# A stage-by-stage fp32 network on one core: convolution by matrix products, read products shared with GpSimd, high and low halves formed from PSUM

## What is computed

```python
def _L1_ffn_ref:      # stage 4: shared plus chosen units, 12 units of 128 hidden
    h = relu(x @ w1 + b1);  y = h @ w2 + b2        # x masked by the choice for 8 of the 12
def _L3_attn_ref:     # stage 7: the scan
    x = resid * rsqrt(mean(resid^2) + EPS) * norm_w
    skip, xe = x @ skip_w.T, x @ in_w.T            # 256 channels
    xc = causal 4-tap convolution of xe along the tokens, by channel, + conv_b
    xs = silu(xc)
    delta = softplus(xs @ wd1.T @ wd2.T + wd2_b);  A = -exp(A_log)
    Bm, Cm = xs @ wb.T, xs @ wc.T                  # 16 of each a token
    h[e,n] = exp(delta[e] * A[e,n]) * h[e,n] + delta[e] * xs[e] * Bm[n]
    y[e] = sum_n h[e,n] * Cm[n];   y = (y + xs * W_D) * silu(skip);  out = resid + y @ out_w.T
def _L3_ffn_ref:      # stage 8: 8 experts of 512 hidden, every token through every expert
    h = relu(x @ W1[e] + b1[e]);  y = gate[e] * (h @ W2[e] + b2[e])
```

## Time and profile before

| | us |
|---|---|
| median of 3 runs (all: 2960.09, 2961.39, 2972.28) | 2961.39 |
| profiled execution, its own time | 2971.4 |
| its span, first to last instruction | 2969.6 |
| mean granted TensorE clock | 0.911 of full |
| stage 4 | 533 to 706 |
| stage 7, the scan alone | 1820 to 2477 |
| stage 8, the experts alone | 2521 to 2950 |

### The profile page before, as it was taken

One profiled execution on the slowest core, in us unless ns is written; L12 is line 12 of the kernel. 1 busy time (PEld: TensorE's weight loads), 2 busy tenths in 40 slices (PEclk: granted clock), 3 DMA queues, 4 the chain that ended last, 5 costly groups with the idle time before them and its releaser, 6 DMA issues.

```text
span 2969.6 us, 34723 instructions
## 1 busy us (share of the span) xinstructions
PE 2466.0 (83%) x12034; PEld 1751.8 (59%) x12034; DVE 2159.7 (73%) x3859; ACT 1261.5 (42%) x2802; POOL 988.2 (33%) x787
## 2 busy tenths in 40 slices
PE   6677778697999999999699995677777775899998
PEld 2554556576888888888567773222222223667676
DVE  6637556897666666665666664788888897799997
ACT  4221232334444444443355554544444443444444
POOL 1000010232222222222045550444444451466664
PEclk8668899898999999999799996888888898999999
DMA  3000000000000000000100000111111120000001
GB/s 164 0 1 1 1 1 1 1 1 15 1 1 1 1 1 1 1 1 1 58 1 1 1 1 15 54 56 51 50 44 56 58 75 1 1 1 1 1 1 29
DMA packets 25136, 55.56 MB, mean 19 GB/s; under 512 B 2544, under 2 KB 6656, under 8 KB 24448
## 3 DMA queue, kind: packets, MB, share of 16 engines
q1 hardware_dynamic: 24928, 53.32, 5.4%
q0 software_dynamic: 32, 0.02, 0.0%
HBM read 50.96 MB, written 2.36 MB: 18 GB/s over the span
## 4 chain that ended last, share of the span: by engine, by line
PE 46%; DVE 27%; issue 13%; POOL 7%; ACT 6%; DMA 0%; DVEq 0%; POOLq 0%; PEldq 0%; PEld 0%; ACTq 0%; SPq 0%
PE ps L190 43%; DVE TMP L206 5%; DVE TMP L2380 5%; PE ps L197 3%; POOL TMPr L210 3%; POOL XT L210 3%; DVE TMP L209 3%; DVE TMPr L206 3%; ACT TMP L201 2%; DVE TMPr L205 2%; POOL TMP L210 2%; DVE XK L206 1%; ACT TMP L202 1%; DVE TMP L207 1%; ACT TMPr L204 1%
## 5 line engine op out<-in xcount | busy, mean ns | idle before, releaser
L190 PE MATMUL ps<-TMPr 128*128 128x512 f32 (+6 forms) x3976 | 1059.5, 412 | 137.5 <-DVE TMP L206 63.4
L190 PEld LDWEIGHTS ps<-TMPr 128*128 128x128 f32 (+4 forms) x3976 | 734.8, 191 | 498.9 <-issue 151.3
L210 POOL TENSOR_TENSOR TMP<-TMP 128x512 f32<-128x512 f32 (+2 forms) x400 | 461.6, 1169 | 961.2 <-ACT TMP L201 443.9
L190 PE MATMUL ps<-TMP 128*128 128x65 f32 (+4 forms) x4320 | 526.3, 289 | 1.2 <-DVE TMP L205 0.5
L190 PEld LDWEIGHTS ps<-TMP 128*128 128x128 f32 (+3 forms) x4320 | 478.9, 191 | 61.7 <-issue 19.9
L201 ACT ACTIVATE TMP<-ps,W 128x256 f32<-128x256 f32 (+2 forms) x560 | 307.5, 590 | 456.6 <-PE ps L190 227.4
L190 PE MATMUL ps<-TMP,W 128*128 128x512 f32 (+5 forms) x720 | 407.7, 691 | 107.4 <-DVE TMP L209 51.4
L206 DVE TENSOR_TENSOR TMP<-ps,TMP 128x512 f32<-128x512 f32 (+1 forms) x514 | 301.0, 611 | 120.3 <-ACT TMP L201 67.3
L190 PEld LDWEIGHTS ps<-TMP,W 128*128 128x128 f32 (+3 forms) x720 | 130.2, 204 | 289.6 <-issue 213.9
L210 POOL TENSOR_TENSOR TMPr<-XK,TMPr 128x512 fp32r<-128x512 f32 (+1 forms) x132 | 194.7, 1477 | 282.4 <-ACT TMPr L204 282.4
L210 POOL TENSOR_TENSOR TMPr<-TMP,TMPr 128x512 fp32r<-128x512 f32 x96 | 126.6, 1320 | 265.2 <-ACT TMPr L204 265.2
(11 more groups left out here) (172 smaller groups left out, 2924.1 us busy)
## 6 DMA issues: line engine op xcount, KB each, us to landing
TMP<-rows SPq DMA_DIRECT2D x128, 256.0 KB, 3.2
W<-wp SPq DMA_DIRECT2D x1, 4124.0 KB, 13.7
W<-wp SPq DMA_DIRECT2D x1, 3072.0 KB, 25.1
W<-wp SPq DMA_DIRECT2D x1, 2136.5 KB, 18.3
...
```

The costliest lines, as they stand in the source:

```text
L190: return nc.tensor.matmul(out, lhsT, rhs, start=start, stop=stop, **k)
L210: gtt = lambda o, a, b, op: nc.gpsimd.tensor_tensor(o, a, b, op)
```

## The change

It has three parts.

1. **Convolution on TensorE.** The taps are folded into the weights: `Wtap` holds four copies of `in_w`, each multiplied by one tap of each channel (one DMA of the taps and one VectorE product of 1024 columns in the norm stage before the scan). A half's convolution is four fp32 products of shifted columns of `XK` accumulated in PSUM (step "conv", in the same `yield` as "gate"). ScalarE then reads PSUM twice ("conv_out"): `Tanh` with bias, and `Identity` with scale one half and bias. The copies into `xe`, the carried columns and the three taps on VectorE go.
2. **Reading the state.** In the five steps n = 1, 4, 7, 10, 13 of each chunk the read product is on GpSimd, with the row Cm[n] brought to `Cr` (two buffers) by a DMA of its own, issued just ahead of the B row. TensorE's selection falls away in these steps. `rows_d` holds 32 rows a chunk and ScalarE's copy for it has 32 rows, where both had 16.
3. **Stages 4 and 8.** Every unit's relu is on ScalarE and writes the high half at once. Then ScalarE subtracts the bias from the high half into `rb` (`Identity` with the negated bias; in stage 8 every fourth unit has it on VectorE). One VectorE `stt` reads PSUM again and forms the low half, max(PSUM, -b) - `rb`. The PSUM bank is free only after that. GpSimd has no subtraction in units any more.

```diff
+        def sync(e):
+            e.wait_ge(s_fence, 4 * begun)
+            nc.sync.dma_start(Wtap, vecs_d[2:3, :].partition_broadcast(128)).then_inc(s_conv, 16)
...
+            e.wait_ge(s_conv, 16)
+            tt(g3(Wtap, 4), g3(Wtap, 4), w("inT").unsqueeze(1).to_broadcast([128, 4, 256]), ALU.mult).then_inc(*taps_ready("taps"))
...
+        by_pool = lambda g: g % 16 % 3 == 1
...
             yield [("open", (i, 0))]
-            yield [("gate", (i, 0))]
-            yield [("last", (i, 0)), ("open", (i, 1))]
-            yield [("shut", (i, 0)), ("gate", (i, 1))]
-            yield [("last", (i, 1))]
+            yield [("gate", (i, 0)), ("conv", (i, 0))]
+            yield [("conv_out", (i, 0))]
+            yield [("shut", (i, 0)), ("open", (i, 1))]
+            yield [("gate", (i, 1)), ("conv", (i, 1))]
+            yield [("conv_out", (i, 1))]
             yield [("shut", (i, 1)), ("rank", i)]
...
-                    bank_free(e, "in", a)
-                    mm(bank("in", a), tile(inT, x), ch(XK, i)).then_inc(*in_pe(a))
+                elif step == "conv":
+                    i, x = a
+                    bank_free(e, "conv", a)
+                    for back in range(4):
+                        o = 512 * i - back
+                        wt = Wtap[:, (3 - back) * 256 + 128 * x:(3 - back) * 256 + 128 * x + 128]
+                        if i % 2:
+                            r = mm(pr, wt, XK[:, o:o + 512], back == 0, back == 3)
+                        else:
+                            r = mm(pr[:, back:512], wt, XK[:, 512 * i:o + 512], back == 0, back == 3)
...
-                elif step == "decay":
+                elif step == "decay" and not by_pool(a):
...
+                elif step == "conv_out":
+                    i, x = a
+                    e.wait_ge(*cv_pe.at(a))
+                    set_free(e, i)
+                    act(ch(sets[i % 2][1], x), pr, ACT.Tanh, scale=0.5, bias=cb[:, x:x + 1]).then_inc(*xt_act(a))
                     if i:
                         e.wait_ge(*dl_dve.at(i - 1))
-                    act(ch(ev, x), xe[x][:, 0:512], ACT.Identity, scale=cw[:, 4 * x:4 * x + 1], bias=cb[:, x:x + 1]).then_inc(*cv_act(a))
+                    act(ch(ev, x), pr, ACT.Identity, scale=0.5, bias=cb[:, x:x + 1]).then_inc(*ev_act(a))
...
-                    e.wait_ge(*cv_act.at(a))
-                    tap(a, 1).then_inc(*t1_dve(a))
-                    e.wait_ge(*t1_dve.at(a))
-                    tap(a, 2).then_inc(*t2_dve(a))
...
-                    for x in range(2):
+                    for x in range(0 if by_pool(a) else 2):
...
+                elif step == "body" and by_pool(a):
+                    k = pool_turn[a]
+                    e.wait_ge(s_row_c[k % 2], 16 * (k // 2 + 1))
+                    for x in range(2):
+                        q = 2 * a + x
+                        e.wait_ge(*h_dve.at((a, x)))
+                        if a >= 2:
+                            e.wait_ge(*y_pe.at((a - 2, x)))
+                        gtt(Cb[q % 4], Cr[k % 2], Hb[q % 4], ALU.mult).then_inc(*hc_pool((a, x)))
...
+                        if k >= 2:
+                            e.wait_ge(*hc_pool.at((by_turn[k - 2], 1)))
+                        nc.sync.dma_start(Cr[k % 2], rows_d[i, 16 + n:17 + n, :].partition_broadcast(128)).then_inc(s_row_c[k % 2], 16)
```

The same edit in stage 4 (stage 8 has it with `B1`, `nB1` and its own names, and with `ts` on VectorE where `a[3] == 3`):

```diff
-                        e.wait_ge(*relu(back(a, 5)))
+                        e.wait_ge(*low.at(back(a, 5)))
...
+                    act(hb[nth[a] % 6][0], PS[nth[a] % 5], ACT.Relu, bias=bias1(a[1])).then_inc(*high(a))
+                elif step == "parts":
+                    e.wait_ge(*high.at(a))
...
+                    act(rb[nth[a] % 4], hb[nth[a] % 6][0].bitcast(F32), ACT.Identity, bias=nbias(a[1])).then_inc(*q_act(a))
...
+                    stt(hb[nth[a] % 6][1], PS[nth[a] % 5], nbias(a[1]), rb[nth[a] % 4], ALU.max, ALU.subtract).then_inc(*low(a))
```

More of the change, by code:

```diff
@@ L163, in build @@
     s_fence, s_eps = lone("s_fence"), lone("s_eps")
+    s_conv = lone("s_conv")
     s_row, s_row_in = [lone(f"s_row{j}") for j in range(2)], [lone(f"s_row_in{j}") for j in range(4)]
-    rows_d = nc.dram_tensor("rows", (NCH, 16, CH), F32).ap()
+    s_row_c = [lone(f"s_row_c{j}") for j in range(2)]
+    rows_d = nc.dram_tensor("rows", (NCH, 32, CH), F32).ap()
     base = (nc.sbuf_base + 63) // 64 * 64
@@ L1277, in stage4 @@
         back = lambda a, n: order[nth[a] - n]
-        wsum = Sig(sem("s4_sums"), ("gate", "gate high", "gate low", "b2a", "b2"))
+        wsum = Sig(sem("s4_sums"), ("gate", "gate high", "gate low", "b2a", "b2", "nb a", "nb"))
         wpart = Sig(sem("s4_weights"), [(n, s, k) for n in units for s in (0, 1) for k in ("high", "low")])
@@ L1284, in stage4 @@
         up_pe = Sig(sem("s4_up"), order)
-        odd = lambda a: a[1] % 2 == 1
-        r_act, r_dve = Sig(sem("s4_relu_act"), [a for a in order if not odd(a)]), Sig(sem("s4_relu_dve"), [a for a in order if odd(a)])
-        c_act, c_dve = Sig(sem("s4_high_act"), [a for a in order if odd(a)]), Sig(sem("s4_high_dve"), [a for a in order if not odd(a)])
-        third = lambda a: a[1] % 4 == 3
-        s_pool, s_dve = Sig(sem("s4_low_pool"), [a for a in order if third(a)]), Sig(sem("s4_low_dve"), [a for a in order if not third(a)])
+        high, low = Sig(sem("s4_high"), order), Sig(sem("s4_low"), order)
+        q_act = Sig(sem("s4_high_unbiased"), order)
         dn_pe, y_dve = Sig(sem("s4_down"), order), Sig(sem("s4_added"), range(NCH))
-        relu = lambda a: (r_dve if odd(a) else r_act).at(a)
-        high = lambda a: (c_act if odd(a) else c_dve).at(a)
-        low = lambda a: (s_pool if third(a) else s_dve).at(a)
         def pe(e):
@@ L1406, in pool @@
                     gtt(l0x, xl.bitcast(F32), l1x.bitcast(F32), ALU.subtract).then_inc(*l0(a))
-                elif step == "parts" and third(a):
-                    h, l = hb[nth[a] % 6]
-                    e.wait_ge(*high(a))
-                    gtt(l, rb[nth[a] % 4], h.bitcast(F32), ALU.subtract).then_inc(*s_pool(a))
         return dict(pe=pe, dve=dve, act=scalar, pool=pool)
@@ L1929, in expert_stage @@
         bank0 = turns([(s, a) for s, a in plan if s in ("gate", "row")], 1)
-        low = lambda a: (mo_lpool if odd(a) else mo_ldve).at(a)
-        high = lambda a: (mo_hact if k == 6 or odd(a) else mo_hdve).at(a)
+        low = lambda a: (mo_lpool if k == 6 and odd(a) else mo_ldve).at(a)
+        nB1 = SM[:, 340:372]
+        unit = lambda a: slice(4 * a[1] + a[3], 4 * a[1] + a[3] + 1)
         def bank0_free(e, s, a):
@@ L1967, in pe @@
                         if nth[a] >= 5:
-                            o = back(a, 5)
-                            e.wait_ge(*(mo_rdve if odd(o) else mo_ract).at(o))
+                            e.wait_ge(*low(back(a, 5)))
                         mm3(ups[nth[a] % 5], (tile(wh, c), tile(wl, c)), xs).then_inc(*mo_up(a))
@@ L2052, in pool @@
             for step, a in plan:
-                if step == "parts" and odd(a):
+                if step == "parts" and k == 6 and odd(a):
                     h, l = hb[nth[a] % NH]
-                    e.wait_ge(*high(a))
-                    gtt(l, fb[nth[a] % 3] if k == 6 else rb[nth[a] % 4], h.bitcast(F32), ALU.subtract).then_inc(*mo_lpool(a))
+                    e.wait_ge(*mo_high.at(a))
+                    gtt(l, fb[nth[a] % 3], h.bitcast(F32), ALU.subtract).then_inc(*mo_lpool(a))
                 elif step == "down" and a[3] == nd - 1:
@@ L2185, in scan_stage @@
         GE = [(g, e) for g in G for e in range(2)]
[L2186 to L2187 removed]
+        c_pe, raw_act = Sig(sem("s7_c_pe"), [g for g in G if not by_pool(g)]), Sig(sem("s7_b_rows"), I)
+        a_act, u_pool, h_dve, y_pe = (Sig(sem("s7_" + n), GE) for n in ("decay", "input", "state", "y_sum"))
+        hc_dve, hc_pool = (Sig(sem("s7_read_" + n), [(g, e) for g, e in GE if by_pool(g) == p]) for n, p in (("dve", False), ("pool", True)))
+        read = lambda g, x: (hc_pool if by_pool(g) else hc_dve).at((g, x))
         c_act = Sig(sem("s7_carried"), [(g, e) for g, e in GE if g // 16 % 2 == 0])
```

198 lines of the change are left out of this document (89 added, 109 removed).

## The result

The changed kernel takes 2851.4 us (median of 4 runs, 2846.7 to 2854.7) and the kernel before, on the same chip, 2966.8 (2960.1 to 2979.5): a ratio of 0.9605, 95% interval 0.9565 to 0.9645. The profiled execution took 2854.7, with a span of 2852.9 and a mean granted clock of 0.917. Run once more, on another chip, the same kernel gave 0.9574 (0.9554 to 0.9594), so differences of 0.3% between two kernels say little.

A forecast was written before the change was run, and what follows sets the result against it. VectorE was taken to lead in stage 4 and the scan, with TensorE nearly full in stage 8. Scan -84, stage 4 -11, stage 8 -17 took 2971.4 to 2859, lowered for run spread to 2855 us; range 2815 to 2912.

The forecast's parts named there:

- The scan: -84 forecast: Scan: seven chunks 12.0 us shorter each, the last 5.9 shorter, the first preparation 6 longer; -84 us together.
- Collisions, +2.4 forecast: Scan: VectorE instructions with two SBUF inputs lengthen beside GpSimd, both shut and half for dx; +2.4 us a chunk.
- TensorE, +1.0: Scan: the convolution's four fp32 products delay the sums VectorE needs, at low clock; +1.0 us a chunk.
- ScalarE, +1.2: Scan, softplus at step 12: VectorE's cover loses the read product pair of step 13; +1.2 us a chunk.
- GpSimd, 48 a chunk: Scan: GpSimd's products at 1.09 and dx at 2.35 make 48 us of the new chunk, so it has room.
- The start, +6: Scan's first preparation, uncovered at low clock: more fp32 products, tap folding, a first C row; +6 us, between 0 and +12.
- Stage 4: -11 forecast: Stage 4: TensorE stays first and its seven holes of 1.67 go, -11.7, with +0.5 back; -11 us.
- stages 4 and 8 give nothing: Rival, chance 0.08: ScalarE's work reaches TensorE's in stage 4, or the copy-from-PSUM-first rule holds; 2884 to 2887 us.
- Stage 8: -17 forecast: Stage 8: seven experts' pairs of TensorE holes go, -13.7, and waits for ScalarE's copy shrink, -3.5; -17.2 us.
- All of it: Rival, chance 0.2: nothing comes back in the scan, as collisions don't coincide, the clock rises and ScalarE hides; 2826 us.
- TensorE sets the pace: Rival, chance 0.17: in the scan's preparation TensorE's convolutions delay the sums, a chunk gives 6 and not 12; 2897 us.
- Slower: Rival, chance 0.04: TensorE stays at 1.2 GHz in the scan, selections and sums queue behind "conv"; 3128 us.

The follow-up runs named there:

- e9: The changed kernel, unedited, run again on another chip; ratio to the kernel before 0.9574, 2844.0 us.
- e4: The changed kernel with six unused SBUF columns ahead of d1, moving B's rows and U 6 columns off dx modulo 512; 0.9578, 2848.6 us.
- e6: The changed kernel with both inputs of all GpSimd products 6 columns apart modulo 512; 0.9577, 2844.2 us.
- e7: The changed kernel with B's four buffers 1, 8, 64 and 256 columns off dx, C's two at 0 and 6 off the state; no time given.
- e12: The changed kernel with GpSimd's read products at steps 2, 5, 8 and 11 only, buffers left in place; 0.9603, 2857.3 us.
- e1: The kernel before with only the convolution moved to TensorE, every read product on VectorE, stages 4 and 8 as before; 0.9761, 2901.6 us.
- e5: The changed kernel with GpSimd's read products at steps 2, 5, 8, 11 and 14; 0.9649, 2865.7 us.
- e8: The changed kernel with GpSimd's read products at steps 2, 5, 8, 11 and 14 and its products' inputs 6 columns apart; 0.9567, 2841.7 us.
- e10: The changed kernel with GpSimd's read products at steps 2, 5, 8 and 11 and its products' inputs 6 columns apart; 0.9528, 2832.5 us.
- e11: The changed kernel with GpSimd's read products at steps 2, 4, 6, 8 and 11 and its products' inputs 6 columns apart; 0.9592, 2852.4 us.

## Why the prediction was right, and where its terms were off

The forecast was 2855, the time 2851.4; the sum against the profiled execution was 2859, that execution took 2854.7. That it came so near is partly luck: several terms were off, and their errors cancel, as the parts below show.

**The scan: -84 forecast, -87.4 measured.** Seven chunk periods fell from 546.4 to 462.8, 83.6, against 84.0, but not as forecast: the first gave 6.1 (75.1 to 69.0), the other six 12.9 each and not 12.0. The last chunk gave 3.8 and not 5.9, the start 0 and not -6. Inside a later chunk, what goes is right to a tenth: read products 5.9 (5.9), taps 4.3 (4.2), holes 6.6 (6.5). Of what comes back:

- *Collisions, +2.4 forecast:* the four `stt` 1.6 and the dx addition 0.7 (busy time per chunk before and after), 2.3 together, but spread otherwise than I had it. I took 0.95 for each of two shut and nothing for the gate; each shut took 0.2 to 0.8 more and each gate 0.3 to 0.4. That the sum fits is luck. One collision in full, VectorE's row above and two of GpSimd's below:

```profile
2134.19 1.51 DVE L211 SCALAR_TENSOR_TENSOR TMP<-TMP 128x512 f32<-128x512 f32 x1
2133.89 1.26 POOL L212 TENSOR_TENSOR TMP<-TMP 128x512 f32<-128x512 f32 x1 [1.56 <-PE ps L192]
2135.11 1.72 POOL L212 TENSOR_TENSOR TMP<-TMP 128x512 f32<-128x512 f32 x1
```

  The `stt` starts at 2134.19 and lasts to 2135.70, 0.55 after GpSimd's running product has ended at 2135.15; GpSimd's next product takes 0.46 longer. The Trainium skill, SBUF — State Buffer, section Who interferes with whom, calls this an exclusive lock that the second comer waits for during the whole instruction; the trace agrees. So do nearly all collisions in the kept traces: of 215 such `stt` that start 0.15 us or more before the end of a GpSimd product, 211 end 0.55 after it, within 0.01. So the usual price is what remains of GpSimd's product, less 0.14.

  Once in the changed kernel it was far more. In the first chunk, GpSimd had work for six products in a row (second row), and the shut of step 4, which began 0.19 before the first of them ended, waited for all the others, too:

```profile
1862.28 6.87 DVE L211 SCALAR_TENSOR_TENSOR TMP<-TMP 128x512 f32<-128x512 f32 x1 [1.17 <-ACT TMP L203]
1861.21 7.39 POOL L212 TENSOR_TENSOR TMP<-TMP 128x512 f32<-128x512 f32 x6
```

  These 6.2 us are about what the first chunk's gain fell short of the others' by (6.8). The same shut took 6.9 in e9 and 4.3 to 6.2 in e4, e6, e7 and e12, but 0.7 to 1.9 in e1, e5, e8, e10 and e11. The lock alone, held for one instruction, doesn't account for this; why VectorE isn't let in between two products isn't shown.

- *TensorE, +1.0, and ScalarE, +1.2:* VectorE's idle time outside the holes that went rose from 1.5 to 3.2 a chunk, 1.7 for the two. The place was wrong. The convolution's four products never held VectorE up (e1 waits 0.3 a chunk for TensorE in all), and softplus cost 0.4. The 1.4 are the result's addition at step 1, which waits for TensorE's output product in a step that lost its pair; in e1, where the step has its pair, that hole is 0.1. I had costed the lost pair at step 13 and not at step 1.
- *GpSimd, 48 a chunk:* 57. The duration of 1.09 was taken over from the earlier trace rows although the change moved the buffers. With these steps that cost nothing that could be measured (e6); with others it cost 24 us (e5 against e8) and 22 to 25 (e12 against e10).
- *The start, +6:* from the stage's beginning to the first scan it took 43.7 before and 43.6 after.

**Stage 4: -11 forecast, -18.3 measured.** The mechanism is the one forecast; TensorE's timeline, before and after, shows why it is larger.

```profile
563.94 10.76 PE L190 MATMUL ps<-TMPr 128*128 128x512 f32 x39 [2.47 <-DVE TMPr L206]
```

```profile
552.78 8.44 PE L192 MATMUL ps<-TMPr 128*128 128x512 f32 x36 [0.58 <-POOL TMPr L212]
561.43 9.16 PE L192 MATMUL ps<-TMPr 128*128 128x512 f32 x39 [0.21 <-DVE TMPr L211]
```

39 products took 10.76 behind the hole of 2.47 and 9.50 behind the holes of 1.67; without a hole they take 9.16. The first hole was followed by seven products 0.43 apart instead of 0.23, at a granted clock of 0.50, and each of the others by three products 0.34 to 0.46 apart at the full clock; what held these up isn't shown, and the view counts it as busy time. I had summed the holes alone (six of 1.67 and that of 2.47 are 12.5) and missed 4.6 in the products (127.2 to 122.6 in that group). "These holes are all that stages 4 and 8 can give" was the step that failed here. ScalarE worked 124 us there, 15.5 a chunk, and didn't reach TensorE, so the rival "stages 4 and 8 give nothing" fell with its rule on copying first: with PSUM read twice, VectorE worked 116.9 us instead of 160.5.

**Stage 8: -17 forecast, -10.6 measured.** TensorE's waits in the experts (total, times, longest), before and then after, and a row of its timeline after:

```profile
PE ps L197 <- ACT XK L204: 9.7, 7, 1.6
PE ps L190 <- POOL TMPr L210: 9.2, 7, 2.2
PE ps L190 <- DVE TMPr L206: 4.7, 6, 0.8
```

```profile
PE ps L199 <- ACT XK L206: 6.5, 7, 1.6
PE ps L192 <- DVE TMPr L211: 6.2, 7, 0.9
```

```profile
2646.58 49.71 PE L192 MATMUL ps<-TMPr 128*128 128x512 f32 x200 [0.92 <-DVE TMPr L211]
```

ScalarE's part gave 3.2 against 3.5 forecast. The wait for GpSimd's low half went, but where the pair of holes (0.79 and 1.17) had been, one of 0.92 stayed in each of six experts, for a low half that now comes behind relu, unbiased copy and `stt`. I had counted both as gone, and in seven experts where the trace of before has the pair in six: 13.7 forecast, and what the pair gave is 6 x 1.03 = 6.2. A last hole of 2.2 ahead of the stage's end, which I hadn't counted, fell to 0.6. The errors of the two stages, 7 too little and 7 too much, cancel, and that is luck.

**The rivals.** "All of it" fell: collisions are real. "TensorE sets the pace" fell: its clock in the scan rose from 0.85 to 0.88 and chunks were 66. "Slower" had nothing for it. The times of the rivals don't start from one base (2826 and 3128 from 2971.4, 2884 and 2897 from 2855), which changes none of these answers.

**The signs.** Of what was to show it right, these came: VectorE first in the scan, chunks of 66, no hole ahead of shut, the clock, ScalarE's 15 a chunk in stage 4. These didn't, or in part: shut took 1.17 us in the mean and not 1.6, GpSimd worked 57 and not 48, and a hole of 0.92 an expert stayed in stage 8. One sign of being wrong came in small: VectorE waits 1.4 a chunk for a product of TensorE.
